# The low-order key products of a cross-attention kernel as one 2 by 2 block product with seven factors

## The reference

```python
q = (x @ Wq).reshape(B, Nq, HEADS, DIM_HEAD)
k = (context @ Wk).reshape(B, context.shape[1], HEADS, DIM_HEAD)
v = (context @ Wv).reshape(B, context.shape[1], HEADS, DIM_HEAD)
sim = jnp.einsum('bihd,bjhd->bhij', q, k) * SCALE
attn = jax.nn.softmax(sim, axis=-1)
out = jnp.einsum('bhij,bjhd->bihd', attn, v)
```

## Time and profile before

| | |
|---|---|
| median of 3 runs | 931.0 us |
| the profiled execution: time, span | 930.53 us, 928.5 us |
| PE busy, matmuls | 905.2 us (97%), 7470 |
| DVE busy | 570.3 us (61%) |
| ACT busy | 639.5 us (69%) |
| POOL busy | 519.0 us (56%) |
| granted PE clock | 1.00 in all of the 40 slices |
| chain that ended last | PE 82%, POOL 5%, DVE 5%, ACT 4% |

### The profile page before, as it was taken

How to read it: one execution, slowest core, us unless ns; L and a number is a source line. 1 busy time by engine, 2 the same in 40 slices (tenths; PEclk the granted TensorE clock), 3 DMA queues, 4 the chain that set the end, 5 groups by cost and what they waited for, 6 DMA issues and landing times.

```text
span 928.5 us, 20113 instructions
## 1 busy us (share of the span) xinstructions
PE 905.2 (97%) x7470; PEld 565.0 (61%) x7470; DVE 570.3 (61%) x1021; ACT 639.5 (69%) x1462; POOL 519.0 (56%) x377
## 2 busy tenths in 40 slices
PE   6899999999999999999999999999899999999998
PEld 4546666666666666666666666666566455544444
DVE  6635656555565555566556555655766779886634
ACT  4658778877778788878878877888777523336540
POOL 4436666556655665665566566778977865310000
PEclk9999999999999999999999999999999999999999
DMA  9348667776777776667577776988799753233502
GB/s 335 98 80 174 132 128 141 139 145 135 153 142 135 126 149 131 140 129 144 129 126 144 168 144 116 207 168 156 157 190 164 120 116 78 46 107 77 181 12 80
DMA packets 340270, 126.38 MB, mean 136 GB/s; under 512 B 316112, under 2 KB 317904, under 8 KB 340176
## 3 DMA queue, kind: packets, MB, share of 16 engines
q1 hardware_dynamic: 324432, 95.09, 55.3%
q10 hardware_dynamic: 15744, 30.02, 10.2%
HBM read 45.36 MB, written 2.10 MB: 51 GB/s over the span
## 4 chain that ended last, share of the span: by engine, by line
PE 82%; POOL 5%; DVE 5%; ACT 4%; issue 2%; DMA 1%; SPq 1%; POOLq 0%; DVEq 0%; ACTq 0%
PE v_ps L657 24%; PE k_ps L657 23%; PE e_ps L726 8%; PE e_ps L657 7%; PE o_ps L746 5%; PE e_ps L1011 3%; PE o_ps L749 3%; POOL p_l L1982 2%; PE o_ps L1004 2%; PE o_ps L765 2%; PE e_ps L1004 1%; ACT p_h L1189 1%; DVE q_max L1524 1%; ACT p_f L1191 1%; POOL acc L2001 1%
## 5 line engine op out<-in xcount | busy, mean ns | idle before, releaser
L1982 POOL TENSOR_TENSOR p_l<-p_f,p_h 128x1024 f16<-128x1024 f32 x128 | 274.1, 2141 | 237.1 <-ACT p_f L1191 236.9
L1189 ACT ACTIVATE p_h<-e_ps,bias 128x512 f16<-128x512 f32 x256 | 175.8, 687 | 3.8 <-issue 1.5
L1191 ACT ACTIVATE p_f<-e_ps,bias 128x512 f32<-128x512 f32 x256 | 176.5, 690 | 0.0
L1519 DVE TENSOR_TENSOR k_l<-k_ps,k_h 128x512 f16<-128x512 f32 x128 | 88.4, 691 | 124.1 <-ACT k_h L1151 124.1
L1524 DVE TENSOR_REDUCE q_max<-e_ps 128x2 f32<-128x1024 f32 x128 | 150.8, 1219 | 7.0 <-PE e_ps L726 0.6
L1512 DVE TENSOR_TENSOR v<-v_ps,v 128x512 f16<-128x512 f32 x127 | 87.6, 690 | 94.2 <-ACT v L1143 94.2
L657 PE MATMUL v_ps<-wv_h,ctx_h 128*128 128x256 f16 x756 | 124.2, 273 | 8.5 <-DVE v L1512 8.5
L657 PE MATMUL v_ps<-wv_l,ctx_h 128*128 128x256 f16 x756 | 123.7, 273 | 0.0
L657 PE MATMUL v_ps<-wv_h,ctx_l 128*128 128x256 f16 x756 | 123.7, 273 | 0.0
L746 PE MATMUL o_ps<-v,pt_h 128*128 128x128 f16 x1024 | 104.2, 220 | 1.3 <-issue 1.3
L657 PE MATMUL k_ps<-ctx_h,wk_h 128*128 128x512 f16 x384 | 103.8, 379 | 0.6 <-DVE k_l L1519 0.6
(11 more groups left out here) (315 smaller groups left out, 1418.1 us busy)
## 6 DMA issues: line engine op xcount, KB each, us to landing
raw<-in_ctx_t ACTq DMA_DIRECT2D x28, 768.0 KB, 5.3
w_raw<-in_w_t SPq DMA_DIRECT2D x32, 256.0 KB, 4.1
raw<-in_ctx_t SPq DMA_DIRECT2D x3, 768.0 KB, 8.6
pt_h<-p_h SPq DMA_TRANSPOSE x128, 3.7
pt_l<-p_l SPq DMA_TRANSPOSE x128, 3.3
out<-xr SPq DMA_DIRECT2D x7, 256.0 KB, 2.0
x_in<-in_x SPq DMA_DIRECT2D x6, 256.0 KB, 11.0
o_all<-in_x ACTq DMA_DIRECT2D x6, 256.0 KB, 3.9
```

The lines of the kernel that those rows point to most:

```text
L1189: act.activation(p_h[:, s % H_RING, h, :], e_ps[s % 2][:, h, :], ACT.Exp, scale=EXP_SCALE, bias=bias[:, m, i, c, 1 + t:2 + t]).then_inc(p_ ...
L1191: act.activation(p_f[:, s % F_RING, h, :], e_ps[s % 2][:, h, :], ACT.Exp, scale=EXP_SCALE, bias=bias[:, m, i, c, 1 + t:2 + t], accum_out=p ...
L1519: dve.tensor_tensor(k_l[:, g % 2, d, t, :], k_ps[:, :], k_h[:, g % 2, d, t, :], ALU.subtract).then_inc(k_split, 1)
L1982: pool.tensor_tensor(p_l[:, s % L_RING, :, :], p_f[:, s % F_RING, :, :], p_h[:, s % H_RING, :, :], ALU.subtract).then_inc(p_split, 1)
```

## The change

A group's key tiles are K[d, t] = Wh[d] Xh[t] + Wl[d] Xh[t] + Wh[d] Xl[t], with d for the pair of heads, t for the quarter, and h and l for the halves. The two trailing products are a 2 by 2 block matrix (Wl[d], Wh[d]) times a 2 by 2 block matrix (Xh[t]; Xl[t]): eight block products of three matmuls. The change makes them with seven block products over sums of blocks. That is done for slots 8 to 111; the others keep `key_quarter`.

- DVE makes five sums of weights once (T1 to T4, `key_sum`), and for each half batch (eight slots) two sums of tokens, S1 and S2; POOL makes S3 and S4.
- PE gathers the high product in a second bank (`o_ps[1]`, called `y_bank_of_keys`) and the shared sums in `k_ps`. At the start of step 1 of a group (s % 4 == 1) it issues six products ahead (`combined_keys_ahead`); the fifth block product goes into the y bank, ACT copies it to SBUF (`keep_key_p5`), and DVE adds it to the y bank in step 2.
- In steps 0 to 2 the low half is two passes on DVE: y minus its high half into `k_rest`, then `k_ps` plus `k_rest`. Step 3 keeps one pass.
- The weighted values now use the one bank `o_ps[0]`, so those of slot s wait for the accumulation of slot s - 1 (before: s - 2). On PE they come behind the scores, on DVE the accumulation of odd slots comes ahead of the maxima.
- The low half of two key weight columns moves from DVE to POOL (`last_keys_low`), the load of later weights waits for the last combined keys, and several semaphores are shared under other counts.

```diff
+        def combined(s):
+            return 8 <= s < SLOTS - 16
...
+        for hf in range(1, B * 2 - 2):
+            for which, step in ((S1, 8 * hf - 4), (S2, 8 * hf - 2), (S3, 8 * hf - 4), (S4, 8 * hf - 1)):
+                if hf == 1:
+                    step = {S1: 5, S2: 6, S3: 5, S4: 7}[which]
+                SUMS_BEHIND.setdefault(step, []).append((hf, which))
...
+            def combined_keys_ahead(s):
...
+                pe.wait_ge(k_split, s)
+                pe.wait_ge(sums_low, sums_at(s // 8) + 2)
+                key_products_of(y_bank_of_keys, k_sum(T1), sums[:, S1, :, :], first=True).then_inc(key_p5_filled, 1)
+                key_products_of(x_bank, k_sum(T2), sums[:, S2, :, :])
...
+                if s % 4 == 0:
+                    pe.wait_ge(ctx_split, ctx_parts(2 * (s // 8)))
+                    key_products_of(x_bank, w(wk_l, 0), h0, first=True)
+                    key_products_of(y_bank_of_keys, w(wk_h, 0), h0, first=True, last=False)
+                    mm = key_products_of(y_bank_of_keys, w(wk_h, 0), l0)
+                elif s % 4 == 1:
+                    pe.wait_ge(key_p5_kept, p5_at(s) + 1)
+                    pe.wait_ge(sums_high, 2 * (s // 8 - 1) + 2)
+                    key_products_of(y_bank_of_keys, w(wk_h, 1), sums[:, S4, :, :], last=False)
+                    mm = key_products_of(y_bank_of_keys, w(wk_h, 1), h0)
+                elif s % 4 == 2:
+                    pe.wait_ge(ctx_split, ctx_parts(2 * (s // 8) + 1))
+                    key_products_of(x_bank, k_sum(T3), sums[:, S3, :, :])
+                    mm = key_products_of(y_bank_of_keys, w(wk_h, 1), h1, first=True)
+                else:
+                    key_products_of(x_bank, k_sum(T4), l1, last=False)
+                    mm = key_products_of(x_bank, w(wk_h, 0), h1)
+                mm.then_inc(k_filled, 1)
...
-                if s >= 2:
-                    pe.wait_ge(acc_ready, s - 1)
-                elif s == 0:
+                if s:
+                    pe.wait_ge(acc_ready, s)
+                else:
                     pe.wait_ge(q_split, 8)
-                acc_bank = o_ps[s % 2]
+                acc_bank = o_ps[0]
...
+                if s < SLOTS and combined(s) and s % 4 == 1:
+                    combined_keys_ahead(s)
                 if s + 1 < SLOTS:
                     value_tiles(s + 1)
                 if s < SLOTS:
-                    key_quarter(s)
-                if 0 <= s - PV_LAG < SLOTS:
-                    weighted_values(s - PV_LAG)
+                    (combined_keys if combined(s) else key_quarter)(s)
                 if s % 2 == 0 and 2 <= s <= SLOTS:
                     scores(s - 2)
                     scores(s - 1)
+                if 0 <= s - PV_LAG < SLOTS:
+                    weighted_values(s - PV_LAG)
...
+                if combined(s) and s % 4 < 3:
+                    bank = y_bank_of_keys
+                    if s % 4 == 2:
+                        act.wait_ge(key_rest, rests_at(s) + 3)
+                act.activation(k_h[:, g % 2, d, t, :], bank[:, :], ACT.Copy).then_inc(k_hi, 1)
...
+                rest, n = k_rest[:, s % 2, :], rests_at(s) + s % 4
+                if s % 4 == 2:
+                    dve.wait_ge(k_filled, s + 1)
+                    dve.wait_ge(key_p5_kept, p5_at(s) + 1)
+                    dve.tensor_tensor(y_bank_of_keys[:, :], y_bank_of_keys[:, :], key_p5[:, :], ALU.add).then_inc(key_rest, 1)
+                    n += 1
                 dve.wait_ge(k_hi, s + 1)
...
+                dve.tensor_tensor(rest, y_bank_of_keys[:, :], hi, ALU.subtract).then_inc(key_rest, 1)
+                dve.wait_ge(key_rest, n + 1)
+                dve.tensor_tensor(lo, x_bank[:, :], rest, ALU.add).then_inc(k_split, 1)
...
+                    dve.scalar_tensor_tensor(sums[:, S1, :, :], h1, LOW, l1, ALU.mult, ALU.add).then_inc(sums_low, 1)
...
+                    dve.scalar_tensor_tensor(sums[:, S2, :, :], h0, -LOW, sums[:, S1, :, :], ALU.mult, ALU.add).then_inc(sums_low, 1)
...
                 done = s - PV_LAG - 1
+                if s % 2 == 1 and 0 <= done < SLOTS:
+                    accumulate(done)
                 if s % 2 == 1 and 0 <= s - X_LAG < SLOTS:
                     quarter_maximum(s - X_LAG)
                     quarter_maximum(s - X_LAG + 1)
```

More of the change, by code:

```diff
@@ L711, in key_quarter, with key_products_of, key_operands, w @@
                              (lambda c: ch[:, c, :], lambda c: cl[:, c, :]), CC).then_inc(k_filled, 1)
+            def key_products_of(bank, rights, left, first=False, last=True):
+                for c in range(CC):
+                    mm = pe.matmul(bank[:, :], rights(c), left[:, c, :], start=(first and c == 0), stop=(last and c == CC - 1),
+                                   skip_group_check=True)
+                return mm
+            def key_operands(s):
+                hf, m = s // 8, s // 4 % 2
+                halves = [(ctx_h[:, (2 * hf + t) % CTX_RING, :, :], ctx_l[:, (2 * hf + t) % CTX_RING, :, :]) for t in range(2)]
+                def w(half, d):
+                    return lambda c: half[:, c, (2 * m + d) * P:(2 * m + d) * P + P]
+                def k_sum(i):
+                    return lambda c: kt[:, i, c, m, :]
+                return halves, xs[:, hf % 2, :, :, :], w, k_sum
@@ L1068, in _ @@
             pe.wait_ge(h_q8, 2 * HC - 2)
-            pe.wait_ge(x2_ready, B)
+            pe.wait_ge(x1_ready, 2 * B)
             for n in range(3):
@@ L1236, in steady @@
                 ahead, pair = 0 <= x < SLOTS, s % 2 == 1
+                if combined(s) and s % 4 == 1:
+                    keep_key_p5(s)
                 if x == 0:
@@ new lines, in token_sum @@
+            def token_sum(hf, which):
+                h0, l0, h1, l1 = [half[:, (2 * hf + t) % CTX_RING, :, :] for t in range(2) for half in (ctx_h, ctx_l)]
+                sums = xs[:, hf % 2, :, :, :]
+                if which == S1:
+                    dve.wait_ge(ctx_split, ctx_parts(2 * hf + 1))
+                    if hf <= 2:
+                        dve.wait_ge(q_filled, 8)
+                    else:
+                        dve.wait_ge(k_filled, 8 * (hf - 2) + 8)
+                    dve.scalar_tensor_tensor(sums[:, S1, :, :], h1, LOW, l1, ALU.mult, ALU.add).then_inc(sums_low, 1)
+                else:
+                    dve.wait_ge(sums_low, sums_at(hf) + 1)
+                    dve.scalar_tensor_tensor(sums[:, S2, :, :], h0, -LOW, sums[:, S1, :, :], ALU.mult, ALU.add).then_inc(sums_low, 1)
@@ L1611, in steady @@
                     q_low(i)
+                carried = done % 16 in (8, 12)
+                if carried and s + 1 < SLOTS:
+                    v_low(s + 1)
                 if 0 <= done < SLOTS:
-                    accumulate(done)
+                    if s % 2 == 0:
+                        accumulate(done)
                     if done % 4 == 2:
@@ L1617, in steady @@
                         o_reciprocal(done // 4)
-                if 0 < s and s + 1 < SLOTS:
+                if 0 < s and s + 1 < SLOTS and not carried:
                     v_low(s + 1)
@@ L2093, in _ @@
                         x_low(r)
+                if s == 2:
+                    last_keys_low()
                 if s == 7:
                     bias_halves()
+                for hf, which in SUMS_BEHIND.get(s, ()):
+                    if which in (S3, S4):
+                        token_difference(hf, which)
             def add_norm(r):
```

148 lines of the change are left out of this document (115 added, 33 removed).

## The result

The changed kernel takes 1082.9 us (median of four runs, 1080.4 to 1090.3) against 930.9 before: ratio 1.165, with an interval of 1.159 to 1.171. The forecast had the direction right and the size wrong: it said 1025, and its range ended at 1068.

The account below looks back on a forecast made before the run. PE set the pace before; after the change the loop through DVE and ACT would. 930.5 + 40.8 (loop) + 40.8 (S1, S2) + 10 (POOL stall) + 2 (other slots) = 1024, median 1025 us; range 950 to 1068.

Parts of the forecast that it names:

- the loop through DVE and ACT: Chain of waits PE, ACT, DVE once round a group: 22.93 us, against 20.71 if PE never waited.
- The plain group: Group of four slots without S1, S2, normalisation or fade: forecast to last 22.93 us.
- the loop term: Slots 8 to 111: each group 1.57 us longer than the 21.36 in the trace, times 26: 40.8 us added.
- the room of a pair: Slack in the chain from one pair's scores to PE's next value tiles: 0.99 us.
- Thirteen times 3.14 is 40.8 us: S1 and S2 on DVE delay the loop by 1.41 and 1.73 us per eight slots: 40.8 us in all.
- I take 1.73 for both, since in the walk POOL's split ends within 0.2 us of either start: S1 and S2 passes on DVE: 1.73 us each, no wait for a POOL pass counted.
- a rival at 0.07: S1 and S2 each wait for a POOL pass, 1.57 us more on each of 26: 1066 us; chance 0.07.
- The fade: POOL's late fade holds up the key-bank sum: 2.5 us in six groups, 0.5 in seven; 10 us net.
- The 8.5 that I took off: All of PE's earlier waits for DVE's value split, subtracted from the 18.5 us of the POOL stall, leaving 10.
- The cover of the weight sums: Five weight-sum passes in slots 4 and 5, hidden while PE makes later queries: nothing; 5 us if cover gone.
- The other slots: The 24 slots keeping nine matmuls, in the new order: 1.16 over a room of 0.99, twelve pairs, 2 us.

Follow-up runs that it names:

- order alone: The kernel before, still nine key products a slot, with only the changed order of scores, weighted values, accumulation and maxima: 970.3 us.
- all repairs: Changed kernel with S1 and S2 in DVE's gap, maxima ahead of accumulation, earlier fade, earlier first maximum, weight sums and S4 moved: 937.5 us, ratio 1.007 to before.
- the maxima first: The changed kernel with DVE's two maxima of an odd step put ahead of the accumulation, as before the change: 1028.5 us.
- the sums in the gap: The changed kernel with DVE making S1 and S2 in step 0, between accumulation and value split, where it stood idle: 1011.6 us.

## Why the prediction was right and wrong

- **What bounds the kernel: right.** PE set the pace before, and the loop through DVE and ACT does so after. The plain group is 22.69 us for 22.93; the loop term comes to 1.33 x 26 = 35 us for 40.8. The order alone makes 0.43 to 0.51 a pair of it, 0.94 of the 1.33; the walk had the room of a pair at 0.99 where it is 0.85.
- **S1 and S2, the step that failed.** "Thirteen times 3.14 is 40.8 us" measured 68 us for eleven sets, 6.2 a set: a term of 80. My estimate of the parts of a set, from the runs: 3.1 of its own length, as forecast; 1.6 for the block (21 us over 13 sets); 1.4 for the clock (1.25 and 1.63 in the two groups of 16 slots that have a set). The passes themselves were right (1.75 us for 1.73), and so were their places on the loop: with the block and the clock taken away the two groups are 26.71 and 26.19 for 26.57 and 26.07. For the block, what failed is the sentence "I take 1.73 for both, since in the walk POOL's split ends within 0.2 us of either start". The split does (it ends at 493.71 + 2.13 = 495.84, and S1 starts at 496.06); but POOL's next instruction is S3, which the change puts into the same step, and I had costed S3 only as POOL's time. The block was in the prediction as a rival at 0.07, at 1.57 on all 26 passes; it came to 2.7 on 6 of them. The Trainium skill (SBUF — State Buffer, Who interferes with whom) says that such a pair blocks each other until the first is done; the trace agrees in both directions, 4.44 for 1.76 and 4.60 for 3.08.
- **No term for the clock, the second step that failed.** The sum priced a wait of PE at its length. After waits of 2.5 to 3.2 us the value tiles behind them took up to 0.64 for 0.33, at the lower level, on the loop itself: 4.5 us in 16 slots, 29 us. Nothing in the trace of before showed it, since its longest wait for the split was 1.3 us; but the prediction forecast waits longer than any that stood in the slots of before, and kept the clock at 1.00 without a word.
- **The fade: the mechanism right, the size short by the clock.** 2.5 were forecast over the plain group, 4.5 measured; at clock 1.00 it is 2.9 (25.04 against 22.18). The 8.5 that I took off for the waits of before was too much: about 5 of it lay in these slots.
- **The cover of the weight sums: wrong.** "Nothing; if that cover were gone, 5 us": a wait of 5.2 us stands there, and slot 8 starts 4.9 later. PE had work there, but DVE's accumulation was queued behind the passes, which took up to 3.33 us beside POOL, and behind the first S1. In the run with all repairs, with the last three passes between the query splits and S1 behind the accumulation, slot 8 starts at 71.5 us, no later than before.
- **The other slots: 2 us forecast, 13.0 measured** (4.8 and 8.2). The order alone brings 4.0 and 6.9 of that. In the rest of the program PE waits 3.99 and 2.08 us for accumulations; only the order was shown as its cause, not which of its moves.

For the profiled execution the terms now come near the whole: 35 of the loop, 41 of the sums at their own length, 21 of the block, 29 of the clock, some 19 of the fades (2.9 x 6.5), 5 + 13 outside, less the 5 by which the groups of before were themselves over 21.36 in the mean (560.3 / 26 = 21.55): 158 for 159.7. Several of these are read from runs with other edits, so the close fit is no proof of each.

**Open:** the changed kernel's runs spread from 1080.4 to 1090.3 us, those with the maxima first as widely, the others less. Two causes are possible. S1 and S3 start 0.05 to 0.5 us apart, and who comes first may change from run to run. Or the clock falls after more of the waits in some runs: with the maxima first S1 is never blocked in the profiled execution, and in both kernels the two slower runs have the lower mean clock (0.956 and 0.957 against 0.960 and 0.962; 0.972 and 0.975 against 0.982). Only one execution of each was profiled, so this wasn't shown.

## What to carry to other kernels

When a change saves matmuls by putting passes on another engine, draw the loop of waits that goes through that engine, and put each new pass where its queue already stands idle: the same passes cost 71 us less in a gap of the same queue. Price a forecast wait of PE by its length and by what the clock does to the work behind it, above all if it is longer than any wait in the trace at hand. For each new pass on VectorE, name what GpSimd does in that very moment, the other new passes included.

## What the hardware showed that I had not expected

- Work that is thrown away made the kernel faster: 13 matmuls in a wait kept the clock at 1.00, and the group fell from 27.81 to 26.19 us.
- In the changed kernel the value tiles kept their full pace after waits of 0.93 and 1.27 us, and with the sums in the gap after 1.79; after 2.52 to 3.22 us they fell to the lower level, at once or up to 1.2 us into the block. With the maxima first, a wait of 2.34 us did one or the other.
- Between S1 on DVE and S3 on POOL, the one that starts first isn't slowed at all (1.76 and 3.08 us), and the other waits it out, even where they start 0.1 us apart.
